# Sorting the edges of a graph network on chip by packed keys instead of by scattered records, with the relation table built beside the sort

## The reference

```
seg = edge_dst * 40 + edge_type
S   = segment_sum(h[edge_src], seg).reshape(n, 40, 128)
agg = einsum('nrd,rdf->nf', S, relation_weights) + cnt @ rFeatures
h   = relu(agg * norm + (agg * norm) @ loop_weight)
```

## Time and profile before

| | before |
|---|---|
| time, median of 3 runs | 9096.4 us (9090.16 to 9111.19) |
| span of the profiled execution | 9046.9 us |
| median less this span | 49.5 us |
| PE busy | 5679.9 us, 63% of the span |
| DVE busy | 5810.5 us, 64% |
| ACT busy | 2292.8 us, 25% |
| POOL busy | 6454.7 us, 71% |
| mean granted TensorE clock | 0.733 of full speed |

### The profile page before, as it was taken

The page is one execution under the profiler, slowest core; times in us unless marked ns, Lnnn a source line. Parts: engine busy times, 40 slices in busy tenths (PEclk is TensorE's granted clock), DMA queues, the critical chain, the costliest instruction groups (busy, mean ns, idle before and its releaser), DMA issues. The chain is left out here.

```text
span 9046.9 us, 131904 instructions
## 1 busy us (share of the span) xinstructions
PE 5679.9 (63%) x35786; PEld 4627.8 (51%) x35874; DVE 5810.5 (64%) x15100; ACT 2292.8 (25%) x3456; POOL 6454.7 (71%) x5675
## 2 busy tenths in 40 slices
PE   0990024444488887698344442555559898989896
PEld 0440023333333333566333332555549898989896
DVE  9660035555577666556444446555559898989898
ACT  2000000000100000343222222222226565656564
POOL 4777767777377776674677772777758787878785
PEclk6995555555655555899666666887769999999998
DMA  1780035555599999895333342444457676767674
GB/s 40 289 308 2 2 84 131 131 131 131 101 213 211 210 210 183 263 290 168 88 82 81 80 73 67 128 129 128 130 118 221 191 221 189 219 190 222 190 221 142
DMA packets 1122974, 1403.89 MB, mean 155 GB/s; under 512 B 276858, under 2 KB 948302, under 8 KB 1109198
## 3 DMA queue, kind: packets, MB, share of 16 engines
q1 hardware_dynamic: 968942, 1098.82, 40.7%
q0 software_dynamic: 153312, 296.65, 17.0%
HBM read 1010.93 MB, written 383.96 MB: 154 GB/s over the span
## 5 line engine op out<-in xcount | busy, mean ns | idle before, releaser
L2437 PE MATMUL ps<-u,wide_r 128*128 x9280 | 1140.5, 277 | 129.3 <-issue 88.6
L2268 POOL TENSOR_TENSOR msg_r<-zo_r,share_r 128x1024 f32<-128x1024 f32 x580 | 1123.1, 1936 | 101.7 <-DVE share_r L2327 46.1
L2437 PEld LDWEIGHTS ps<-u,wide_r 128*128 128x128 f32 x9280 | 1092.2, 193 | 131.3 <-issue 131.2
L2449 PE MATMUL ps<-msg_r,hots_r 128*128 128x128 f32 x9280 | 1140.7, 276 | 24.4 <-POOL msg_r L2268 23.1
L2010 POOL DMA_INDIRECT z_r<-x_tab,src_row x880 | 854.4, 971 | 417.2 <-issue 268.0
L2449 PEld LDWEIGHTS ps<-msg_r,hots_r 128*128 128x128 f32 x9280 | 1081.8, 192 | 32.9 <-POOL msg_r L2268 31.9
L297 POOL DMA_INDIRECT rec_tab<-pay,row_i x831 | 808.0, 972 | 374.9 <-issue 275.1
L575 POOL DMA_INDIRECT ring<-y_tab,y_row x880 | 838.0, 952 | 306.9 <-issue 266.0
L1172 POOL DMA_INDIRECT ring_m<-t_tab,src_row x880 | 835.3, 949 | 307.9 <-issue 280.8
L1624 POOL DMA_INDIRECT ring_e<-t_tab,src_row x880 | 832.4, 946 | 271.7 <-issue 268.0
L2276 POOL TENSOR_TENSOR prod_r<-prod_r 128x512 f32<-128x512 f32 x580 | 735.0, 1267 | 319.2 <-DVE prod_r L2299 302.9
(11 more groups left out here) (303 smaller groups left out, 10622.4 us busy)
## 6 DMA issues: line engine op xcount, KB each, us to landing
zo_r<-zo_tab SPq DMA_DIRECT2D x2320, 192.0 KB, 2.8
ring_e<-k_tab SPq DMA_DIRECT2D x464, 260.0 KB
k_tab<-ring_m SPq DMA_DIRECT2D x220, 520.0 KB, 6.3
y_tab<-wide SPq DMA_DIRECT2D x100, 1024.0 KB, 3.9
zo_tab<-z_r SPq DMA_DIRECT2D x110, 512.0 KB, 3.6
hot_bytes_e<-hb_tab SPq DMA_DIRECT2D x464, 64.0 KB, 3.3
dl_b<-dl_tab SPq DMA_DIRECT2D x220, 128.0 KB, 3.8
zo_tab<-hot_bytes SPq DMA_DIRECT2D x220, 128.0 KB
```

What stands on the lines that cost most here:

```text
L2268: nc.gpsimd.tensor_tensor(msg[:, g % WR].rearrange("p c (k d) -> p c k d", d=CD), z_of(g).rearrange("p c (k d) -> p c k d", d=CD), share[: ...
L2437: last = nc.tensor.matmul(ps[:, 2 * (g % 2) + c // 4, c % 4 * D:(c % 4 + 1) * D], wide[:, g % WR, c, :], u[:, bass.ds(tiles[g % NO % 4 * O ...
L2449: last = nc.tensor.matmul(ps[:, 4 + g % 2, c // 2 * D:(c // 2 + 1) * D], hots[:, g % WR, c, :], msg[:, g % WR, c, :], start=c % 2 == 0, st ...
```

## The change

The scatter of records, the rank scans and the second phase are gone. Each edge becomes one float key of 32 bits: the target in the sign, the exponent and the upper mantissa (13 bits, shifted by 19), the source (shifted by 6), and the type in the low 6 bits. The exponent never takes the values of infinities or denormals. The target's bits are laid out so that tiles 48 to 25 come first, descending, as negative numbers, and tiles 0 to 24 after them. Blank edges are put in for every tile as it needs (`fill_f`, `fill_ok`). There are 128 x 1024 keys, and VectorE sorts them by a bitonic network of 17 stages, 153 compare steps. Each step is one minimum and one maximum of 128x512 from one key buffer into the other. Descending runs are made by negating keys. Steps that compare between partitions are made on turned keys: `ask` has TensorE transpose all eight 128x128 blocks into PSUM (`turn`), 15 times in all. At the end the key's fields are unpacked in place.

The relation table is made beside this. Its work is cut into 245 units of 1024 columns. Units with m % 3 == 1 are added by VectorE straight from PSUM; for the others ScalarE copies PSUM to SBUF and POOL adds the relation row in place. How far the table runs in step with the sort is written out by quotas: half a unit for each counted tile from the 25th on, one for each compare step, two for each turn, four with the keys, and the rest behind the small tables.

```diff
-            eq = wide[:].bitcast(u8)[:, 0:NT * EJP].rearrange("p (t j) -> p t j", t=NT)
+            rf_b = sb("rf_b", [P, R * D], fp32, ph)
+            y_out = sb("y_out", [P, YS, UW], fp32, ph)
+            keys = [sb(f"keys_{n}", [P, KEYS], fp32, ph) for n in range(2)]
...
+            def by_vector(m):
+                return m % 3 == 1
...
+            COUNT_UNITS, STEP_UNITS, TURN_UNITS = 0.5, 1.0, 2.0
...
+                    def y_add(m):
+                        dve.wait_ge(s_y, m + 1)
+                        if m >= YS:
+                            dve.wait_ge(s_yo[m % YS], 16 * (m // YS))
+                        v.tensor_tensor(y_out[:, m % YS, :], made(m), added(m), ALU.add).then_inc(s_yd, 1)
+
+                    def y_adds(units):
+                        quota[0] = min(quota[0] + units, UNITS)
+                        while done[0] < int(quota[0]):
+                            if by_vector(done[0]):
+                                if done[0] < 3:
+                                    dve.wait_ge(s_rf, 16)
+                                y_add(done[0])
+                            done[0] += 1
...
-                    for t in range(NT):
-                        v.tensor_scalar(eq[:, t, :], tile_b[:], float(t), None, ALU.is_equal).then_inc(s_hot, 1)
+                    for k in range(NT):
+                        if k >= 2:
+                            dve.wait_ge(s_cnt, k - 1)
+                        v.tensor_scalar(junk[:, k % 2, :], tile_b[:], float(bucket_at(k)), None, ALU.is_equal, ALU.add,
+                                        accum_out=cnt[:, k:k + 1]).then_inc(s_cnt, 1)
+                        if k >= 24:
+                            y_adds(COUNT_UNITS)
...
-                    def scan(t, a, b, out):
-                        v.tensor_tensor_scan(out, one.broadcast_to([P, b - a]), eq[:, t, a:b], base[:, t:t + 1],
-                                             ALU.mult, ALU.add).then_inc(s_scan, 1)
...
+                    def compare(view):
+
+                        lo, hi = view(keys[at[0]][:])
+                        to_lo, to_hi = view(keys[1 - at[0]][:])
+                        note(v.tensor_tensor(to_lo, lo, hi, ALU.min))
+                        note(v.tensor_tensor(to_hi, lo, hi, ALU.max))
+                        at[0] = 1 - at[0]
+                        y_adds(STEP_UNITS)
+                        follow()
...
+                    def ask():
+                        v.nop().then_inc(s_ask, 1)
+                        mark(("turn", turns[0]))
+                        turns[0] += 1
+                        y_adds(TURN_UNITS)
+                        dve.wait_ge(s_turn, turns[0])
...
-                    for j in range(EJ):
-                        if j == 0:
-                            pool.wait_ge(s_row, 1)
-                        if j == CUT:
-                            pool.wait_ge(s_row, 2)
-                        nc.gpsimd.indirect_dma_start(
-                            out=rec_tab, out_offset=bass.IndirectOffsetOnAxis(ap=row_i[:, j:j + 1], axis=0),
-                            in_=pay[:, j, :], in_offset=None).then_inc(s_sc, 16)
+                    pool.wait_ge(s_rf, 16)
+                    for m in range(UNITS):
+                        if not by_vector(m):
+                            pool.wait_ge(s_ye, other_units(m) + 1)
+                            nc.gpsimd.tensor_tensor(y_out[:, m % YS, :], y_out[:, m % YS, :], added(m), ALU.add)\
+                              .then_inc(s_yp, 1)
...
+                    for m in range(UNITS):
+                        if not by_vector(m):
+                            act.wait_ge(s_y, m + 1)
+                            if m >= YS:
+                                act.wait_ge(s_yo[m % YS], 16 * (m // YS))
+                            nc.scalar.activation(y_out[:, m % YS, :], made(m), ACT.Copy).then_inc(s_ye, 1)
...
+                    def turn(n, at):
+                        products_to(quotas["turn", n])
+                        pe.wait_ge(s_ask, n + 1)
+                        for h in range(BLOCKS):
+                            last = nc.tensor.transpose(turned[:, h * P:(h + 1) * P], keys[at][:, h * P:(h + 1) * P], ident[:])
+                        last.then_inc(s_turn, 1)
```

531 lines of the change are left out of this document (264 added, 267 removed).

## The result

The changed kernel takes 8686.5 us (median of 4 runs, 8670.2 to 8695.8), the kernel before 9098.7 (4 runs beside them, 9090.2 to 9111.2). The profiled execution has a span of 8691.8 us and took 8693.6 as a whole.

What follows compares the result with a forecast made beforehand. POOL's serial scatter set the first phase's end. Sort start 113 us plus 569 (306 + 162 + 60 + 41), then the tail, gave first gather 818 against 1224.1; 406 us less, 8690 us, range 8480 to 8775.

Steps and rivals of the forecast that it cites:

- The start: Loads, 49 bucket counts, four table additions and keys before the sort; sort to start at 113 us, bounds 95 to 135.
- a sign of being wrong: Before the sort: the start held up by stores behind the loads for longer than 20 us would refute the forecast.
- The price of one count: VectorE's accumulating count of 832 elements before the sort: 1025 ns, about 1.1 us with the reading of the sum.
- VectorE's own work: In the sort: 153 steps 207 us, 61 additions 74, turned-key copies 20, negations 5; 306 us.
- Mutual hindrance: In the sort, VectorE's SBUF steps and POOL's additions exclude each other: 2.65 us lost 61 times, 162 us.
- Turns and clock: In the sort: 15 turns of about 4 us, 60 us; TensorE's lower clock, 0.81, another 41 us.
- The second rival: TensorE stays at its lower clock through the sort: 657 us instead of 569, 8778 us; chance 12%.
- Sort: The whole sort beside the table: 306 + 162 + 60 + 41 = 569 us, ending at 682.
- Behind it: After the sort: unpacking and small tables 32 us, 46 units 80 us, last stores 8, 16.1 to first gather at 818.
- The first rival, no hindrance: VectorE and POOL do not hinder each other in the sort; products set the pace, 8488 us; chance 20%.
- The slower rival: Slower than before: new edge order costs the four gather phases over 0.115 us more per gather; chance 3%.
- From the first gather to the time: Later phases unchanged: span 9046.9 - 406 = 8641, plus 49.5 us by which the median exceeds the span, 8690 us.

Runs made afterwards that it cites:

- the last experiment: GpSimd's addition given in turn four forms, addition or multiplication, second operand full or 64 values repeated: 2.35 us with a full row, 1.93 repeated; no kernel time given.
- the last gated version: Gated pairs (GpSimd's addition starts with VectorE's two from PSUM) with 1.3 units for each sort step instead of 1: 8465.8 us, ratio 0.9344.
- the first three edits: Against the changed kernel: no GpSimd addition, ratio 0.9323; all additions by VectorE, 0.9447; two thirds by VectorE, 0.9485.
- the other chip: The changed kernel unchanged, run again on another chip: 8622.6 us against 9041.8 for the kernel before, ratio 0.9537.
- both versions: 1.3 units a step instead of 1, with all additions by VectorE (8508.7 us, ratio 0.9408) and with gated pairs (8465.8 us, 0.9344).

## Why the prediction was right, point by point

**The start: the sum right, by errors that cancel.** The sort begins at 113 us (113). But the targets were used at 35.9 us (forecast 38 to 39), and the 49 counts follow each other at 0.94 us, 46 us in all and not 54, since the reading of the sum falls beside the next count. What filled the gap up again is this row, and with it some 5 us by which GpSimd's additions held up three shifts (2.62 instead of 0.59 us for L320):

```profile
85.56 1.23 DVE L276 TENSOR_TENSOR y_out<-ps,rf_b 128x1024 f32<-128x1024 f32 x1 [8.44 <-DMA y_tab<-y_out]
```

VectorE stood still for 8.44 us until a store of the table had freed its buffer: the first of these stores stands behind the load of the types, whose issue blocked SP's queue for 15.93 us, and so was issued only at 70.79 us. The forecast had named such a wait only as a sign of being wrong, from 20 us on, and had it at nothing in the sum. The price of one count was right: it came from the straight line through the earlier trace rows, 1.025 us, and not from the plain comparison's 0.587. "SBUF — State Buffer" of the Trainium skill (Who interferes with whom) leaves the accumulating form out of the two-port fast modes, and the trace agrees: 1.019 us, and 0.087 for reading the sum.

**VectorE's own work: 18 us too high.** 306 us were forecast. The steps at their undisturbed price are 210 us, the 61 additions 74.4, copies 18.2, negations 4.7: 307.6 us of durations. But where an operation need not wait for the one ahead, it begins some 0.1 us before that one ends, and in the kernel without GpSimd's additions VectorE is busy for 288 us of the sort. The forecast took the overlap into account for the steps alone, and less of it. Only with the 288 does the sum close: 288 + 163 + 100 us idle (95.8 of them waits for TensorE) = 551.

**Mutual hindrance: right in kind; the size right by two errors that cancel.** Forecast 162 us from a single place in the trace of before; the steps lost 365.1 - 210.3 = 155 us and the negations 8, together 163, the steps' mean 1.19 where some 1.2 was named. But GpSimd's addition takes 2.35 us undisturbed, not 1.94: the 1.936 of the earlier trace rows is the price of a form with a repeated operand, as the last experiment shows. For 121 additions (2.58 each in the sort's window) that is 310 us of GpSimd instead of 237. What hid it was more too: 310 - 163 = 147 us of GpSimd cost nothing. I had counted on 74 us beside VectorE's additions; by the trace only 41 us lie there. 56 us fell into times in which VectorE stood idle, 5 beside its copies from PSUM, and of the 210 us beside steps and negations 163 were lost.

**Turns and clock: the sum right, the cause only in part.** 60 + 41 = 101 us were forecast, and VectorE waited 95.8 us, at a granted clock of 0.84 (forecast 0.81). In the kernel without GpSimd's additions, with the same quotas and a clock of 1.00, the waits are 45.3 us, all but 0.9 of it at the 14 turns that lie in the sort (the 15th is behind its last step): 3.2 each where I took 4. The other 50 us hang on the hindrance: TensorE held up by late additions, and its clock lower with it. I had put that on the clock alone (41) and charged it to no one; it belongs to the price of GpSimd's work, which is then 163 + 50 = 213 us. TensorE's two levels are 1.2 and 2.4 GHz; in the changed kernel TensorE stood still for up to 8 us at a time (it was busy for 386 of 551 us) and had 0.84; in the last gated version, busy for 412 of 451 us, and with all additions by VectorE, busy for 357 of 446, it had 1.00. "TensorE: Matmul & The Clock Gate" of the Trainium skill (HAM oscillation) describes a clock that falls in such pauses, and the trace agrees to that extent. The second rival, a clock that stays low, did not come: a mean of 0.84 excludes it.

**Sort: 551 us instead of 569. Behind it: right.** Tables end at 695 (714 - 682 = 32 forecast, 31 measured), the 46 units behind the sort take 82 us of products up to 772.7 (80), which begin 4 us before the tables end, and from there to the first gather it is 25 us (8 + 16). The first gather came at 797.7, forecast 818; 18 of these 20 us are the sort's.

**The first rival, no hindrance: excluded** by the steps' mean in the changed kernel and by the first three edits. That its price, a first gather at 616 us, is near the 617.5 of the last gated version is chance, since that one has another share and quota: gated with the same quota the first gather came at 647.2, without GpSimd's additions at 575.1.

**The slower rival: excluded.** The gathers' phases did not change with the order of the edges: a gather of the attention's first pass takes 946 ns against 949, and the other three passes 1108, 1097 and 1122 us against 1106, 1100 and 1121.

**From the first gather to the time: right by luck.** The first gather came 20 us earlier than I said, 426 instead of 406, but the medians differ by only 412 (9098.7 - 8686.5). 14 us got lost behind the first gather, and with the 2 us by which the median of before was higher in four runs than in three they made the forecast come out 3.5 us off instead of 20. I had added to the span the 49.5 us by which the runs' median exceeded it, as a constant. It is none: in the profiled execution of the changed kernel the time exceeds the span by 1.8 us. The profiled execution of before had the attention's first pass at 1143 us, the fastest seen; if the timed runs on that chip had it near 1199, as the changed kernel's profiled run has, that is about the 49.5 us. No trace of those timed runs exists, so this is argued only, and so is the place of the 14 us. On the other chip, where this pass was 1143 us in the changed kernel, the time is 8622.6, and 1221 to 1224 less 799, 422 to 425 us, explain the 419 us between the two kernels.

**What the gain consists of.** The scatter of 831 records at 1.30 us went, and a sort of 257 us took its place. The overlap with the table, which the profile shows as busy engines everywhere, is worth 19 us in this form; in the last gated version the same overlap is worth 818.0 - 617.5 = 200 us. GpSimd's 121 additions in the sort cost 213 us there; VectorE makes them in 121 x 1.22 = 148 us at the most.

What stays open: how the 50 us of waits divide between products held up by late additions and a clock that is lower for it (no run held the one and changed the other), and why the gathers are slower where GpSimd adds nothing.

## What to carry to other kernels

Before work is given to GpSimd to relieve VectorE, look at what VectorE does in the meantime. If it is two-input work from SBUF, each of GpSimd's operations makes one of VectorE's wait it out, and help can cost as much as it saves: 1.3 us of standing still for an addition that VectorE makes in 1.22. Start GpSimd's operation on the same event as operations of VectorE that read PSUM and last as long, and it is nearly free: 8 us in all here, instead of 81 for as many ungated.

Engines that are all busy don't prove an overlap. Doing the parts one after the other (here 19 us slower) prices it in one run. And a quota between two streams is worth tuning after the hindrance is gone: 0.3 units a step more were 30 us in both versions, since a unit behind the sort costs TensorE's 1.72 us and in the sort only VectorE's share.

When a price is taken from a row, take it from one with the same operands: same shape, engine and type, but with one operand repeated, was 18% too cheap.

## What the runs showed of the hardware

- GpSimd, 128x1024 f32, two operands in SBUF: 2.35 us with two full operands, 1.93 with one of 64 values read 16 times, addition or multiplication alike.
- VectorE with an operand in PSUM ran beside GpSimd without loss on either side: two additions in 2.35 us beside one of GpSimd's in 2.35.
- Not only two-input operations of VectorE wait for GpSimd: the negation L369 took 2.45 us beside it and 0.43 without, and the shifts of the keys L320 and L321 2.62 and 2.68 us, against 0.59 in the kernel with the table behind the sort. The forecast had such operations at 0.6 to 1.0 us.
- But not every operation from SBUF waits: the 49 accumulating counts L306 took 1.009 to 1.022 us, all of them, though 20 of them ran beside GpSimd's additions (two from 90.23 us on, for example), and these kept 2.34 to 2.35 too. The count moves 832 columns in 1.02 us, the shift 831 in 0.59: 0.8 and 1.4 columns a nanosecond. It is the fast one and the two-input one that were held up.
- It goes both ways: GpSimd's addition that began at 100.06 us, into VectorE's two-input operation L317 (99.89 to 100.92), took 3.06 instead of 2.35 us.
- A gather of GpSimd takes 954 to 956 ns in the three kernels in which GpSimd makes no addition in the first phase, 946 to 949 in all others (the attention's first pass), the same code; the cause is open.
- A stage that has the DMA engines busy for 0.97 to 1.00 of its time varied between 1143 and 1199 us with the same work. The difference is 13% of the gain of the change (56 of 419 us), and would have been taken for a cost of the new edge order without the second chip.
